# A graph network kernel whose last token tile gathers expert rows for 98 partitions instead of 128

## The reference

```
x = x + L0_gnn(layernorm(x), edges)      graph convolution, batch norm, gelu, residual
x = x + L0_ffn(layernorm(x))             product-key expert layer (below)
x = x + L1_gnn(layernorm(x), src, dst)   graph convolution with one 512x512 weight
x = x + L1_ffn(layernorm(x))             one of 8 weights, by the bin in which feature 0 falls

L0_ffn, per token:
  for each of 8 heads: the 8 best of 256*256 key pairs -> indices, scores      (64 picks in all)
  inner = x . w_down[index]                                   (64 dot products of length 512)
  vals  = relu(inner) * softmax(scores)
  out   = sum of vals * w_up[index]                           (64 rows of length 512)
```

## Time and profile before

| what | value |
|---|---|
| median of 3 runs | 1358.37 us (1356.52 to 1358.50) |
| profiled execution, device time | 1359.03 us |
| profiled execution, span | 1357.2 us |
| mean granted TensorE clock | 0.966 |
| PE, DVE, ACT, POOL busy | 86%, 70%, 38%, 48% of the span |
| read from HBM | 359.53 MB |

### The profile page before, as it was taken

The page is one execution under the profiler, slowest core; times in us unless marked ns, Lnnn a source line. Parts: engine busy times, 40 slices in busy tenths (PEclk is TensorE's granted clock), DMA queues, the critical chain, the costliest instruction groups (busy, mean ns, idle before and its releaser), DMA issues.

```text
span 1357.2 us, 16428 instructions
## 1 busy us (share of the span) xinstructions
PE 1161.3 (86%) x3844; PEld 566.4 (42%) x3845; DVE 943.7 (70%) x2771; ACT 520.7 (38%) x1280; POOL 654.3 (48%) x706
## 2 busy tenths in 40 slices
PE   0788889996499999899898999989999799889098
PEld 0444445554254444444444444444444233334043
DVE  4777785022669997887978879788797866665211
ACT  1677730053644544344344444434443333320010
POOL 2000000000376677777777776777767777530212
PEclk9999999997599999999999999999999999999599
DMA  8400000000399999999999999999999999943443
GB/s 344 171 1 0 1 1 0 0 0 0 125 410 409 370 409 409 410 408 409 409 408 410 409 409 409 409 409 409 409 409 401 410 409 409 406 159 144 181 149 117
DMA packets 105765, 378.76 MB, mean 279 GB/s; under 512 B 11824, under 2 KB 11826, under 8 KB 104536
## 3 DMA queue, kind: packets, MB, share of 16 engines
q0 software_dynamic: 94720, 343.40, 63.7%
q1 hardware_dynamic: 10968, 34.48, 6.9%
HBM read 359.53 MB, written 19.41 MB: 279 GB/s over the span
## 4 chain that ended last, share of the span: by engine, by line
PE 44%; DVE 15%; DMA 13%; POOL 11%; issue 8%; ACT 5%; DVEq 4%; ACTq 0%; POOLq 0%; SPq 0%
PE tr L1433 17%; DMA AT<-in_wdu,idx 7%; POOL big L511 6%; PE acc L1312 6%; DMA big<-in_wdu,idx 4%; PE acc L1292 4%; POOL AT L511 4%; PE acc L1410 4%; PE acc L1385 3%; DVE big L1116 3%; PE tr L1484 3%; PE tr L1460 3%; DVE outT L846 2%; PE acc L1396 2%; DVE AT L1116 2%
## 5 line engine op out<-in xcount | busy, mean ns | idle before, releaser
L511 POOL DMA_INDIRECT big<-in_wdu,idx x466 | 439.8, 944 | 500.5 <-DVE idx L1056 348.8
L1433 PE MATMUL tr<-big,diag 128*128 128x512 f32 x932 | 434.1, 602 | 34.1 <-ACT diag L736 33.7
L736 ACT ACTIVATE diag<-ident,inner 128x128 f32<-128x128 f32 x640 | 221.6, 393 | 472.0 <-DVE inner L1116 470.6
L1116 DVE CUSTOM_DVE_ANT_0 big<-big,acc,prob 128x512 f32<-128x512 f32 x466 | 327.6, 742 | 79.7 <-DMA big<-in_wdu,idx 78.4
L1433 PEld LDWEIGHTS tr<-big,diag 128*128 128x128 f32 x932 | 168.5, 190 | 258.1 <-issue 166.9
L511 POOL DMA_INDIRECT AT<-in_wdu,idx x174 | 168.7, 970 | 61.6 <-issue 48.7
L1433 PE MATMUL tr<-AT,diag 128*128 128x512 f32 x348 | 163.3, 602 | 8.9 <-ACT diag L736 8.8
L1292 PE MATMUL acc<-outT,diag 128*128 x612 | 120.4, 347 | 40.3 <-DVE outT L846 18.7
L1116 DVE CUSTOM_DVE_ANT_0 AT<-AT,acc,prob 128x512 f32<-128x512 f32 x174 | 122.4, 742 | 33.5 <-DMA AT<-in_wdu,idx 33.1
L846 DVE TENSOR_SCALAR outT<-big 128x1280 f16 x204 | 98.0, 548 | 34.8 <-PE acc L1292 30.0
L1433 PEld LDWEIGHTS tr<-AT,diag 128*128 128x128 f32 x348 | 62.7, 190 | 90.5 <-issue 62.2
(11 more groups left out here) (234 smaller groups left out, 1056.5 us busy)
## 6 DMA issues: line engine op xcount, KB each, us to landing
sorted_rows<-big SPq DMA_DIRECT2D x8, 1280.0 KB, 17.4
big<-in_we SPq DMA_DIRECT2D x8, 1024.0 KB, 15.1
big<-in_wdu,idx POOLq DMA_INDIRECT x466, 10.6
x<-sorted_rows SPq DMA_DIRECT2D x14, 512.5 KB, 3.4
AT<-in_wdu,idx POOLq DMA_INDIRECT x174, 10.8
x<-in_x SPq DMA_DIRECT2D x1, 2304.0 KB
qk<-in_wq SPq DMA_DIRECT2D x1, 2048.0 KB, 19.8
big<-in_w0t SPq DMA_DIRECT2D x1, 1024.0 KB, 27.5
```

Of the source, the lines that this page charges most:

```text
L511: pool.indirect_dma_start(out=k.slot[r * GS + s], out_offset=None, in_=k.wdu_d, in_offset=bass.IndirectOffsetOnAxis(ap=k.idx[i % 2][:, j:j ...
L736: ins = act.activation(k.diag[:, c * P:(c + 1) * P], k.ident[:, :], ACT.Relu, scale=k.inner[:, j:j + 1])
L1116: ins = dve.tensor_tensor_reduce(out=row, in0=row, in1=k.Y[i % 2], scale=k.prob[:, (i % 2) * HK + j:(i % 2) * HK + j + 1], scalar=0.0, op0 ...
L1433: ins = pe.matmul(k.O[i % 2], k.diag[:, c:c + P], row, start=(g == 0 and s == 0), stop=(g == NG - 1 and s == GS - 1))
```

## The change

The gathers of the last tile name 98 partitions of the slot and 98 indices. The other 30 partitions of each slot keep what lies there: rows that tile 8 (or, before the ring has gone round, its last groups) gathered, the first halves multiplied by what was applied to them. DVE, ACT and PE work on all 128 partitions as before.

```diff
@@ -508,9 +508,10 @@
                 pool.wait_ge(k.few_ready, 1)
             for s in range(GS):
                 j = g * GS + s
+                rows = P if i < NT - 1 else LAST
                 pool.indirect_dma_start(
-                    out=k.slot[r * GS + s], out_offset=None, in_=k.wdu_d,
-                    in_offset=bass.IndirectOffsetOnAxis(ap=k.idx[i % 2][:, j:j + 1], axis=0),
+                    out=k.slot[r * GS + s][0:rows], out_offset=None, in_=k.wdu_d,
+                    in_offset=bass.IndirectOffsetOnAxis(ap=k.idx[i % 2][0:rows, j:j + 1], axis=0),
                 ).then_inc(k.landed[r], 16)
```

## The result

The changed kernel takes 1399.57 us (median of 4 runs, 1394.51 to 1400.73) against 1357.89 us before. The ratio is 1.0301, 95% interval 1.0275 to 1.0328. It is 41.7 us slower, where 1348.8 us had been forecast. The profiled execution took 1399.39 us, 40.4 us more than the one before.

A forecast was written before the change was run, and what follows sets the result against it. Gather landings were taken to set the last tile's pace, with PE next. PE's slack 10.3 - 1.0 waits + 0.3 earlier landing gave 9.6 us; 1359.03 - 9.6 = 1349.4, forecast as median 1348.8 us, range 1346.8 to 1355.0.

The forecast's parts named there:

- The landing cadence: Last tile's gathers: 98 rows spread over the engines land in 0.98 us each instead of 1.28, a pair in 1.96.
- the far end: Other end of the landing estimate: the straggling engine keeps its 8 rows and a pair of gathers stays at 2.56 us.
- the three spacings: Possible times between landings of gather pairs in the last tile: 1.96, 2.24 or 2.56 us.
- 1 to 2 for the clock: After the expert layer, where the clock falls in places, the total may shift 1 to 2 us either way.
- Bytes: 64 gathers lose 30 rows of 4096 bytes, 7.86 MB, worth 19.2 us if only transfers stood in the way.
- What comes next, PE: PE's counted work from group 288 to 319 is 71.6 us against 81.9 today, limiting the gain to 10.3 us of slack.
- The 1.0 us of waits: PE's waits on DVE at groups 291 and 298, about 0.5 us each, were expected to stay and reduce the gain.
- POOL: Issuing gathers stays at 0.94 us for 98 rows and stays hidden, because POOL is ahead.
- rival (c): POOL takes longer for a count that isn't a multiple of 16, and its cover is used up: 1368.7 us, chance 0.07.
- The padding rows: All thirty fall into the same bin in the last layer, which still works through 13 tiles and as many rounds.
- The late engine: Near the last tile's end one DMA engine runs some 12 us behind the other fifteen and sets the landings.
- (b): Straggling engine keeps 8 rows, landings stay at 2.56 us a pair: 1358.4 us, no change, chance 0.10.

The follow-up runs named there:

- kdrop_b: Kernel before, last-tile gathers name all 128 partitions but the 30 padding rows' indices are out of bounds and dropped: 1358.45 us, 0.9998 of before.
- m3_drop: Gathers alone, 8 KB rows, 20 each: all 128 54.3 us; second stage, 98 to 127 dropped, 53.7; every fourth dropped 42.0; 98 named 76.9; 96 named 70.8.
- kwait_b: Changed kernel, with POOL waiting at group 288 until all gathers of tile 8 have landed: 1389.75 us, 1.0233 of before.
- kmid_b: Kernel before, with the last tile gathering 64 rows into partitions 32 to 95: 1348.71 us, 0.9926 of before.
- k64: Changed kernel, with the last tile gathering 64 partitions (0 to 63) in place of 98: 1371.08 us, 1.0094 of before.
- m2_places: Gathers alone, 8 KB rows, by place: 64 partitions at 32 to 95 409 GB/s, at 0 to 63 and 64 to 127 210 and 207; 128 and 98 in turn 230.

## Why the prediction was wrong

**The step that failed is "The landing cadence".** It took 98 rows at the full rate, spread over the engines, 0.98 us a gather, and put the unchanged 1.28 us as the far end. Neither end held the truth. At 233 GB/s a gather of 98 rows (0.401 MB) takes 1.72 us. The prediction bounded the cost by how many rows an engine has to move, and never asked where they land. A row then occupies its engine for longer: sixteen engines at 233 GB/s take 0.28 us for 4096 bytes, at 409 GB/s 0.16. The cause, as far as place and count can tell, is that other engines write to the same group of partitions. Even without this queueing there was nothing to gain: partitions 0 to 63 fill eight groups with 8 rows each, and with those rows kept kdrop_b and the second stage of m3_drop are no faster than full gathers.

**The sum by its own terms.** At that rate a pair takes 3.44 us in place of 2.56, 0.88 more, or 28 us over 32 groups. (The first products stand 2.92 us apart from 1140.14 to 1216.02, none of the three spacings that the prediction named, because part of their transfers had run before.) When the first of them is issued at 1099.7, the gathers of tile 8 issued over the 20 us before are still out, some 16. At 233 GB/s each takes 2.25 in place of 1.28 us, together 15.5 us. That makes 44 us at most; 37.9 arrive by the end of the expert layer, where the last groups run at PE's pace again (26.19 of 28.40 us busy from 1215). The 2.5 us after it lie in the part where the prediction allowed 1 to 2 for the clock. That split is an estimate; only the 16 us of kwait_b were measured by an experiment.

**Bytes:** right, 7.87 MB less, and worth nothing.

**What comes next, PE:** right in the main, as kmid_b shows, where the transfers are out of the way (with 64 rows a gather, so it tests only this term and not the 0.98 us). In its 74.44 us PE runs 187 matrix instructions: the 180 counted ones, 71.6 us, and seven that were left over from groups before, 3.0 us at 0.43 each. The 1.0 us of waits that the prediction kept isn't there. That its total, 1348.71 us, meets the forecast of 1348.8 is in part luck: the expert layer ends 10.8 us earlier than before, and 1.1 us of that is lost behind it.

**POOL:** right. 0.94 to 0.95 us for 98 rows, and rival (c), the only one on the slower side, had the wrong place. **The padding rows:** 14 tiles are loaded in the last layer in both traces. The prediction's 13 give 14, since the rounds take four tiles each and the last one two, so the rounds are as many as before, as worked out. **The late engine:** right as read; it stays late in the change, where the transfers run on at 11 GB/s from 1232 to 1240:

```profile
1232.00:1240.00 8.00, 8.00 (x23) 4.18 (x22) 6.57 (x19) 2.77 (x8) 0.00 (x0) 1.00 0.03 11
```

**The rivals.** (b), "no change", was the nearest. What it supposed of the late engine holds where all partitions are named and rows are dropped (kdrop_b), but it took the pace of 8 rows as unchanged when fewer partitions are named. Its sentence that nothing in the trace spoke against it was also the gap. No row showed a gather on other than 128 partitions, so the far end should have reached beyond 1.28 us, and the slower side should have held more than 0.07.

**The clock** is a side effect. From 1121.4 to 1140.1 PE waited for landings, busy 11.96 of 18.74 us, and the granted clock was 0.77 of full; four matrix instructions at the start of it took 3.34 us in place of 1.98:

```profile
1120.10 3.34 PE L1434 MATMUL tr<-AT,diag 128*128 128x512 f32 x4 [4.21 <-ACT diag L737]
```

It should cost little, since the DMA engines stay busy (share 1.03) and PE isn't what ends last there; no run tested that.

**Open.** Which engine wrote which partition isn't in the trace. That engines queue at a group is inferred from place and count alone (kmid_b against k64, m2_places, m3_drop). It doesn't explain why a gather of 98 that is alone takes no longer than a full one. No version that computes the whole was faster than before. Spreading the padding evenly over the groups might be one, by m3_drop, but it needs another order of tokens throughout the kernel and wasn't tried.

## What to carry to other kernels

Don't cut a saturated gather to its first 98 (or 112, 96, 64) partitions to save bytes. The time of a DMA follows its fullest group of partitions and how its engines meet there, and it also slows the full transfers in flight beside it. If rows must go, drop them by index and evenly over the groups; dropped at the end they save next to nothing (53.7 against 54.3 us for 20 gathers). And where no row of a trace shows the new shape, bound its price from the worse side too, or time it alone first.

## What the runs showed of the hardware that was not expected

- 112, 96 and 64 partitions from 0 on run at 212 to 250 GB/s with all 16 engines in use, 128 at 406 to 423. 64 partitions at 32 to 95 run at 409.
- Full and cut gathers in turn run at 230 GB/s, about as the cut ones alone, not at the mean.
- A gather of 97 partitions has, by its packets, all rows on one engine, with some 1470 small packets and 82 GB/s over its stage (share of the engines 0.36, so the gathers in flight don't all lie on the same one), and POOL's instruction takes 2.13 us in place of 0.94:

```profile
357.00:456.00 99.00, 0.00 (x0) 44.13 (x23) 1.00 0.36 82
```

and the gathers of that stage, by line:

```profile
L70 POOL DMA_INDIRECT slots<-in_wdu,idx x22: 944/2133/2162, 357.6 to 455.6; - x22
```
